# Transformer decoder layer on one core: stack loads signalled by halves, unread products in the tail, an earlier value projection, two-tensor forms of the norms and a cast

## The reference

```python
x = x + attn(layernorm(x))                 # 16 heads of 16, rotary, causal
x = x + xattn(layernorm(x), ctx, mask)     # 16 heads of 64, 77 context rows, input mask
x = x + ffn(layernorm(x))                  # 256 -> 1024 -> 256, exact gelu
# each linear of ffn: x @ fake_quant(W).T + b + 2 * (x @ A.T) @ B.T   (rank 16)
layernorm: (x - mean) / sqrt(var + 1e-5)
```

## Time and profile before

| | us |
|---|---|
| median of 3 runs | 640.81 |
| lowest, highest | 640.13, 643.83 |
| the profiled execution | 644.52 |
| its span, first to last instruction | 642.8 |
| mean granted TensorE clock in it | 0.937 |

### The profile page before, as it was taken

One profiled execution on the slowest core, in us unless ns is written; L12 is line 12 of the kernel. 1 busy time (PEld: TensorE's weight loads), 2 busy tenths in 40 slices (PEclk: granted clock), 3 DMA queues, 4 the chain that ended last, 5 costly groups with the idle time before them and its releaser, 6 DMA issues.

```text
span 642.8 us, 11809 instructions
## 1 busy us (share of the span) xinstructions
PE 531.2 (83%) x4334; PEld 451.6 (70%) x4334; DVE 392.6 (61%) x1093; ACT 301.7 (47%) x484; POOL 250.1 (39%) x317
## 2 busy tenths in 40 slices
PE   2388779778987989889979997999899799958955
PEld 2376657656666777878778776878887687847755
DVE  4757531867858943796489539946963683554332
ACT  2333364331544745166445654672755167426323
POOL 5820022644453363155262517262454006522210
PEclk9689999976988979899999999999999799988969
DMA  5589999943210523042224222226140501111000
GB/s 187 168 237 184 189 206 238 283 131 128 71 51 1 160 55 88 8 152 64 75 75 121 71 71 87 75 59 119 51 112 3 155 22 41 37 41 37 1 16 17
DMA packets 63709, 62.45 MB, mean 97 GB/s; under 512 B 6868, under 2 KB 60804, under 8 KB 63652
## 3 DMA queue, kind: packets, MB, share of 16 engines
q1 hardware_dynamic: 62148, 56.74, 33.9%
q0 software_dynamic: 1504, 4.95, 2.2%
HBM read 38.28 MB, written 23.10 MB: 95 GB/s over the span
## 4 chain that ended last, share of the span: by engine, by line
PE 52%; DVE 19%; ACT 9%; DMA 7%; issue 5%; POOL 4%; SPq 3%; DVEq 0%; ACTq 0%; POOLq 0%
PE banks L797 8%; PE banks L798 7%; PE banks L799 7%; PE banks L955 5%; DVE banks L2379 4%; PE banks L1057 4%; PE banks L1046 4%; PE banks L932 4%; PE banks L1119 3%; DMA k_stack<-rot_dram 3%; DMA fold_raw<-fold_dram 2%; PE banks L969 2%; ACT probs L1749 2%; DMA fold_dram<-work 2%; PE banks L831 1%
## 5 line engine op out<-in xcount | busy, mean ns | idle before, releaser
L2379 DVE CUSTOM_DVE_ANT_0 banks<-banks,causal_qk 128x256 f32<-128x256 f32 (+1 forms) x256 | 84.0, 385 | 19.5 <-PE banks L932 17.8
L564 POOL TENSOR_TENSOR work<-work,rc 128x616 f32<-128x616 f32 x32 | 40.5, 1265 | 103.1 <-DVE rc L2479 103.1
L581 POOL TENSOR_SCALAR_AFFINE_SELECT probs<-probs 128x256 f32<-128x256 f32 x128 | 53.2, 442 | 65.4 <-ACT probs L1749 65.3
L571 POOL TENSOR_TENSOR fold_lo<-fold_raw,fold_hi 128x616 fp32r<-128x616 f32 x32 | 48.7, 1524 | 47.5 <-ACT fold_hi L1717 47.5
L1717 ACT ACTIVATE work<-banks 77x512 f32<-77x512 f32 (+1 forms) x72 | 43.2, 601 | 48.9 <-PE banks L1046 45.4
L1749 ACT ACTIVATE probs<-banks 128x768 f32<-128x768 f32 x64 | 51.8, 809 | 29.8 <-PE banks L955 29.3
L932 PE MATMUL banks<-k_stack,q_stack 96*128 96x256 f32 (+1 forms) x256 | 42.9, 293 | 19.9 <-DVE mneg L2379 9.2
L2477 DVE TENSOR_REDUCE sm<-work 128x8 f32<-128x616 f32 x32 | 25.4, 793 | 50.8 <-ACT work L1779 50.7
L932 PEld LDWEIGHTS banks<-k_stack,q_stack 96*128 96x128 f32 x256 | 37.1, 202 | 26.6 <-DVE mneg L2379 11.3
L2334 DVE TENSOR_TENSOR late<-banks,late 128x512 fp32r<-128x512 f32 x40 | 27.4, 685 | 38.0 <-ACT late L1717 38.0
L955 PE MATMUL banks<-q_stack,k_stack 100*128 100x128 f32 (+1 forms) x256 | 46.1, 303 | 5.1 <-ACT probs L1749 2.3
(11 more groups left out here) (190 smaller groups left out, 1569.5 us busy)
## 6 DMA issues: line engine op xcount, KB each, us to landing
fold_raw<-fold_dram SPq DMA_DIRECT2D x32, 308.0 KB, 3.0
fold_dram<-work SPq DMA_DIRECT2D x8, 616.0 KB, 8.3
rot_dram<-rot_s_hi SPq DMA_DIRECT2D x16, 256.0 KB, 2.8
rot_dram<-rot_s_lo SPq DMA_DIRECT2D x16, 256.0 KB, 3.4
q_stack<-rot_dram SPq DMA_DIRECT2D x32, 128.0 KB, 2.7
k_stack<-rot_dram SPq DMA_DIRECT2D x32, 128.0 KB, 3.0
fold_dram<-fold_raw SPq DMA_DIRECT2D x4, 616.0 KB, 6.1
fold_dram<-fold_raw_hi SPq DMA_DIRECT2D x4, 616.0 KB, 9.0
```

Of the source, the lines that this page charges most:

```text
L571: pool.tensor_tensor(fold[1][:, :, g % 2], raw[:, :, g % 2], fold[0][:, :, g % 2].bitcast(F32), ALU.subtract).then_inc(g_lo, 1)
L581: last = pool.affine_select(out=diagonal, in_=diagonal, compare_op=ALU.is_ge, fill=0.0, base=0, pattern=[[0, 2], [1, P]], channel_multipli ...
L2379: last = dve.tensor_tensor_reduce(out=held[:, at], in0=held[:, at], in1=bias, scale=-1.0, scalar=HUGE, op0=ALU.add, op1=ALU.min, accum_out ...
```

## The change

1. `stack_ld` becomes two semaphores, one for each half (8 DMAs each). `scores(a, 0)` waits for the first, `scores(a, 4)` for the second, `store_rotated` for both.
2. A new PE function `fill(at, count)` issues `count` products of 128x128 weights by 256 columns into a bank that nothing reads. Six calls, 82 products in all, stand in the tail.
3. `project_v(0)` moves ahead of `keys(0, 0)` in PE's list.
4. `norm` uses `scalar_tensor_tensor` with the mean as the scalar and the inverse deviation as a second tensor, broadcast over 256 columns. The result is the same.
5. The cast in `split_max` becomes `tensor_tensor` with max of the tensor and itself.

```diff
-        rot_st, stack_ld = sem("rot_st"), sem("stack_ld")
+        rot_st, stack_ld = sem("rot_st"), [sem("stack_ld0"), sem("stack_ld1")]
-        STACK_DMAS = 16
+        STACK_DMAS = 8
...
             def store_rotated(n):
-                sp.wait_ge(stack_ld, 16 * STACK_DMAS * n)
+                for done in stack_ld:
+                    sp.wait_ge(done, 16 * STACK_DMAS * n)
...
-                                     rows[p, :, part]).then_inc(stack_ld, 16)
+                                     rows[p, :, part]).then_inc(stack_ld[half], 16)
...
-                                     rows[p, 0:DH, part]).then_inc(stack_ld, 16)
+                                     rows[p, 0:DH, part]).then_inc(stack_ld[half], 16)
...
                 if g == 0:
-                    pe.wait_ge(stack_ld, 16 * STACK_DMAS * (a + 1))
+                    pe.wait_ge(stack_ld[0], 16 * STACK_DMAS * (a + 1))
...
+                if g == 4:
+                    pe.wait_ge(stack_ld[1], 16 * STACK_DMAS * (a + 1))
...
+            def fill(at, count):
+                for _ in range(count):
+                    pe.matmul(halves(at)[:, 0, :], wqkv[0][:, 0, 0:P], wqkv[0][:, 0, 0:W], start=True, stop=True)
...
             project(0, 1)
+            project_v(0)
             keys(0, 0)
-            project_v(0)
             transpose_a(1)
...
             output2(6, 3)
+            fill(2, 24)
             transpose_b(7)
             transpose_f(6)
             scores2(7, 0)
             narrow(6)
             hidden(6, 0)
             hidden(6, 1)
+            fill(2, 14)
             hidden(6, 2)
...
             output2(7, 3)
+            fill(2, 28)
             transpose_f(7)
+            fill(2, 8)
             narrow(7)
+            fill(2, 4)
             hidden(7, 0)
             hidden(7, 1)
             hidden(7, 2)
             hidden(7, 3)
+            fill(2, 4)
             project_down(7, 0)
...
                 for q in range(QT):
-                    last = dve.tensor_scalar(xn[:, q, :], src[:, q, :], mv[:, q, 0:1], rs[:, q, :],
-                                             ALU.subtract, ALU.mult)
+                    last = dve.scalar_tensor_tensor(out=xn[:, q, :], in0=src[:, q, :], scalar=mv[:, q, 0:1],
+                                                    in1=rs[:, q, :].broadcast_to([P, D]),
+                                                    op0=ALU.subtract, op1=ALU.mult)
...
-                dve.tensor_copy(mneg_s[:, half, :, :, 0, :], mneg[:, :, :, part]).then_inc(m_split, 1)
+                dve.tensor_tensor(mneg_s[:, half, :, :, 0, :], mneg[:, :, :, part], mneg[:, :, :, part],
+                                  ALU.max).then_inc(m_split, 1)
```

## The result

The changed kernel takes 638.46 us (median; 636.46 to 641.86), the kernel before 641.1 us. The ratio is 0.9962, with a 95% interval of 0.9945 to 0.998: 2.4 us faster, between 1.3 and 3.5. The forecast was 7.1 us. The profiled execution took 638.55 us, with a span of 636.8. Ratios leave out the few slow executions, over 1.5% above the fastest of their kernel, while medians here take all.

What follows compares the result with a forecast made beforehand. No single engine bounds the kernel: its chain passes back and forth, TensorE holding 52% and VectorE 19%. Terms -2.6 - 2.4 - 3.4 + 1.3 = -7.1 us from the median 640.8 gave 633.7 us, range 627 to 640.

Steps and rivals of the forecast that it cites:

- stack halves: PE's waits for stack loads before scores of elements 1 and 7 go: 2.6 and 2.4 us saved.
- products: Unread products in PE's tail delay nothing and keep the granted clock at 1.0: 3.4 us saved, at most 4.4.
- value projection: At the start, its 12 products move into an idle stretch before keys(0, 0): zero, at best a gain of 1 us.
- norms: L2329 on VectorE: the two-tensor form lengthens norms in the chain, +1.3 us; bounds +4.9 and a gain of 13.7.
- cast: VectorE's cast of the maxima takes 175 ns in either form: zero.
- The holds: VectorE's norms and cast, held behind GpSimd instructions, were expected to stay held in the two-tensor form.
- The rival in which they vanish: Norms and cast on VectorE: two-tensor forms aren't held behind GpSimd, time 618.7 us; chance 0.07.
- Element 1: Scores there start nearly 3 us earlier; VectorE's 2.1 us idle before the first maxima goes, plus 0.5 from the clock.
- Element 7: Scores no longer wait for the second half; transpose_b(6) moves from 509.55 to its norm's end at 507.1: 2.4 us.
- I subtract the same from the median.: The profiled execution's 644.5 us was 3.7 above the median 640.8; the 7.1 us gain was taken from the median: 633.7.
- Given back at the next junction: VectorE arrives earlier beside a long GpSimd instruction and a new hold costs 3.7 us: 637.4 us; chance 0.15.
- Slower: the broadcast second tensor is slow: L2329, 18 chain instructions: over 0.88 us each eats the other 8.4 us; at 1.2 us, 646.6 us; chance 0.04.

Runs made afterwards that it cites:

- The seven pairs doubled: On the kernel before, norm_b of elements 3, 5, 7 and norm_f of 0, 3, 4, 7 computed twice: 11.5 us slower (7.6 to 15.3).
- the experiment that was to test it: On the kernel before, the other nine norm pairs of the two later stages, taken as outside the chain, computed twice: 5.6 us slower (3.1 to 8.0).

## Why the prediction was wrong

The forecast was a gain of 7.1 us, and 2.4 came. Term by term, against the edits alone:

| term | forecast | alone (interval) |
|---|---|---|
| stack halves | -2.6 - 2.4 = -5.0 | -3.7 (-5.4 to -2.1) |
| products | -3.4 | -3.0 (-4.9 to -1.0) |
| value projection | 0 | +0.8 (-0.8 to +2.4) |
| norms | +1.3 | +3.1 (+1.3 to +4.9); with the cast +4.1 (+2.2 to +6.1) |
| cast | 0 | +0.3 (-1.9 to +2.4) |
| sum | -7.1 | -1.8 (halves, products, value, and norms with cast) |
| sum without the forms | -8.4 | -5.9; measured together -9.4 (-11.9 to -6.9) and -9.3 (-12.8 to -5.8) |

The sum of the parts alone is -1.8, within the whole's interval, but two differences cancel in it: together, halves, products and value projection gave more than the -5.9 of their sum, and beside them the forms cost 7.0 to 7.6 us, more than the 4.1 alone. Neither difference is clear of its intervals. Either way the -8.4 forecast for the rest was near what was measured, and the miss lies in the forms.

- **The failed step is the price of the norms**, the term of +1.3 us, "0.05 us for the first norm of each of 9 pairs and 0.13 for each of 7 held ones". Alone the norms cost 3.1 us, in the whole the forms cost 7.0 and 7.6. Three things in it were off. *The price of one.* The form costs 0.07 us for an instruction, so 0.15 for a pair, about three times the 0.05; the 0.13 for a held norm was near (4217 against 4109, 1487 against 1358, 1698 against 1565: 0.11 to 0.13). The nine pairs grew by 1.8 us. *The count.* "About 18 norm instructions stand in the chain": they are 22. The view of the whole chain had left out its shorter pieces, and with the two pairs missed the growth is 2.1 us. The same slip is in the runs' comparison: the pieces of L2342 in the changed kernel's whole chain sum to 18.8 us against 15.8 before, +3.0, where those of 0.7 us and over alone have 15.9 against 14.4. *The rate.* The term took each microsecond in the chain to cost one. The seven pairs doubled passed on 1.7 (1.15 to 2.3). The first and second are read from the traces; the third, and whatever makes the forms dearer beside halves and products, is measured without its cause. One difference is seen there: with the halves, `norm_b(0)` and a norm of `norm_f(5)` stand in the chain as well (halves alone, and both profiles of the whole). The +4.9 that the prediction held as the upper bound covers the norms alone, and not what the forms cost in the whole.
- **The holds** stayed, as argued from the earlier trace rows. The rival in which they vanish is dead. The Trainium skill, in "SBUF — State Buffer", section "Who interferes with whom", has both kinds of form contend with GpSimd; the trace agrees, with 4.22 us for the held norm.
- **The rate of the form.** The Trainium skill, in "VectorE: DVE Perf Modes", section "The perf-mode tier table (the rule you actually need)", led to an estimate of 0.13 us more for each norm. Measured are 0.07 (479 against 408 ns): half of it, and more than the 0.01 that the statistics' row gave.
- **Element 1.** The mechanism is right. In 11 of the 13 profiles without halves PE waits 1.7 to 4.9 us for `k_stack`; in the other two (both forms alone, the cross attention's norms twice) it comes too late to wait. In the seven with halves nothing waits for a stack. Counted from the start of `norm_b(0)`, `scores(1, 0)` starts after 6.8 to 7.0 us with halves and after 7.0 to 10.8 without, 9.2 on average. The first maxima start after 8.2 us on average with halves and 10.3 without: 2.1 us, as forecast.
- **Element 7.** The mechanism is right: the transpose behind the scores waits for its norm, and the idle stretch is gone. In the seven profiles with halves `transpose_b(6)` starts 0.06 us after that norm's end, in the 13 without 0.6 to 2.5 us after it, with a median of 1.8. The forecast 2.4 was read from the profile with the longest of these waits. So some 0.6 us of the -5.0 were too many; the rest of the distance to -3.7 is within the interval.
- **Products.** Right in kind: none delays anything, and the windows are at 1.0. One part was mistaken on the safe side: "Two idle pieces of over 1 us remain around the transposes". The level held through them. One stretch of 3.4 us at the lower level is left, from 583, behind the second group (mean clock 0.58 from 583 to 587).
- **Value projection.** Zero, as far as a measurement tells.
- **"I subtract the same from the median."** Right to do: the profiled execution of before was 3.4 us over the median.
- **Rivals.** "Given back at the next junction" gave the nearest time (637.4), for a reason that no run shows: without the forms the parts keep at least their gains beside each other. That nearness is luck. "Slower: the broadcast second tensor is slow" had the right place, L2329, with a threshold of 0.88 us that presumed 18 instructions; the form takes 0.48.

## What to carry to other kernels

Read the chain whole before counting in it, and expect pairs just outside it to enter once they are delayed. A view that shows its longest pieces leaves out short instructions, and an edit that touches every tile lives in those: here two of eleven pairs were missed, first in the forecast and then in the experiment that was to test it. Take the new form's time from a run or bound it by its worst row, since 0.15 us for each of 24 pairs outweighed a removed stall of 3 us. A microsecond put into such a chain cost 1.7 at the end, so one for one is not a safe rate. Measure a bundle's parts alone, and the bundle without each, before keeping all of it: here one edit hid more than half of what the others gave.

## What the runs showed of the hardware

- **A delay can cost more than itself.** Doubled norms of the cross attention passed on 1.3 us for each added, the seven of the chain 1.7. Beside it the granted clock fell. Its mean over the profiled execution was 0.937 before; here are those of the cross attention's norms twice, of the pairs in the chain twice, and of the change without its forms, each with its span:

```profile
core 0: 650.9 us, clock 0.922
```

```profile
core 0: 653.2 us, clock 0.928
```

```profile
core 0: 629.0 us, clock 0.963
```

  The time at the lower level is 2 x (1 - clock) x span: 81 us before (0.937, 642.8), 102 us with the cross attention's norms doubled, 47 us without the forms. Over all executions of each the means are nearer each other: 77, 92 and 52 us. Within 35 executions of the unchanged kernel, a line through time against this number rises by 0.20 us for each microsecond at the lower level (correlation 0.68). By that, 15 us more at the lower level are 3.0 us, which would cover the excess of the doubled norms over what was added (11.4 against 8.6), if all that was added arrived. That the delays cause the lower level, by leaving PE idle more often, is argued and not shown by a run of its own.
- **A held VectorE instruction gets in between two of GpSimd's.** With GpSimd's 4.51 us instruction in four, the norm pair beside it fell from 4.43 to 2.16 us.
- **The form with a tensor operand more** (`scalar_tensor_tensor` for `tensor_scalar`) takes 0.07 us more over 256 float32 columns (479 against 408 ns). `tensor_tensor` in place of the cast takes nothing that can be seen more over 16 columns (176 against 175 ns).
